# A two-layer graph network: the second layer's edge inputs laid out and loaded another way

## What is computed

```
hid = silu(edge_scalars @ fc_w1 / 8)           # edge_scalars: 100000 x 64
w   = hid @ fc_w2 / 8                          # 224 weights an edge
es, ev = h_s[src], h_v[src]                    # row src of the node table
y0, y1 = edge_attr[:, 0], edge_attr[:, 1:4]    # four factors an edge
m   = products of w, es, ev, y0 and y1         # 96 scalars, 128 vectors an edge
agg = segment_sum(m, dst)                      # over the edges of each node
```

## Time and profile before

| | us |
|---|---|
| median of 3 runs | 4200.96 |
| lowest and highest | 4200.42 and 4204.09 |
| span of the profiled execution (core 0, first to last instruction) | 4499.2 |
| PE busy in that span | 3588.3 |
| VectorE busy | 3413.8 |
| ACT busy | 3129.9 |
| POOL busy | 3025.2 |
| DMA moved, all queues | 411.01 MB |

### The profile page before, as it was taken

One profiled execution on the slowest core, in us unless ns is written; L12 is line 12 of the kernel. 1 busy time (PEld: TensorE's weight loads), 2 busy tenths in 40 slices (PEclk: granted clock), 3 DMA queues, 4 the chain that ended last, 5 costly groups with the idle time before them and its releaser, 6 DMA issues. The chain is left out here.

```text
span 4499.2 us, 96352 instructions
## 1 busy us (share of the span) xinstructions
PE 3588.3 (80%) x21340; PEld 2740.0 (61%) x21340; DVE 3413.8 (76%) x12346; ACT 3129.9 (70%) x11217; POOL 3025.2 (67%) x2469
## 2 busy tenths in 40 slices
PE   3888887887778888888778866976888888888887
PEld 3777777777777777777777766864333333333334
DVE  5777777777777777777777787875777777777775
ACT  4777777777777777777777765745666666666664
POOL 2888888888888888888888851113666666666662
PEclk7999999999999999999999998987899999999989
DMA  4443344334334334333433348962333333333333
...
DMA packets 374905, 411.01 MB, mean 91 GB/s; under 512 B 98580, under 2 KB 322580, under 8 KB 374580
## 3 DMA queue, kind: packets, MB, share of 16 engines
...
## 5 line engine op out<-in xcount | busy, mean ns | idle before, releaser
L668 POOL DMA_INDIRECT ACC<-dst_tab,idx x784 | 1308.6, 1669 | 238.9 <-issue 238.9
L733 POOL DMA_INDIRECT ACC<-hid_tab,idx x784 | 830.4, 1059 | 554.7 <-issue 352.8
L812 PE MATMUL TR<-ident,M 128*128 128x128 f32 x4704 | 675.2, 281 | 445.5 <-DVE M L1533 345.6
L657 POOL DMA_INDIRECT ACC<-src_tab,idx x784 | 790.0, 1008 | 312.7 <-issue 217.5
L812 PEld LDWEIGHTS TR<-ident,M 128*128 128x128 f32 x4704 | 525.3, 143 | 539.2 <-DVE M L1533 422.8
L1136 ACT ACTIVATE MT<-TR 128x768 f32<-128x768 f32 x784 | 600.8, 825 | 26.8 <-PE TR L812 17.8
L1125 ACT ACTIVATE ACC<-W,ACC 128x64 f32<-128x64 f32 x2352 | 571.6, 327 | 0.0
L1318 ACT ACTIVATE ACC<-TR,y 128x128 f32<-128x128 f32 (+1 forms) x1568 | 419.7, 460 | 195.5 <-remote 100.3
L861 PE MATMUL HP<-w_hv,MT 128*128 128x128 f32 x3136 | 536.5, 295 | 0.0
L836 PE MATMUL E<-w_mv,MT 128*128 128x128 f32 x3136 | 477.6, 275 | 0.0
L1009 PE MATMUL HP<-M,ohE 128*128 128x480 f32 x800 | 408.0, 636 | 43.2 <-DVE M L1856 29.9
...
## 6 DMA issues: line engine op xcount, KB each, us to landing
h_tab<-ACC SPq DMA_DIRECT2D x392, 160.0 KB
...
ACC<-src_tab,idx POOLq DMA_INDIRECT x784
ACC<-dst_tab,idx POOLq DMA_INDIRECT x784
ACC<-hid_tab,idx POOLq DMA_INDIRECT x784
...
```

Of the source, the lines that this page charges most:

```text
L657: pool.indirect_dma_start(gat0[:, v.slot8, g, :], None, src_tab.ap(), bass.IndirectOffsetOnAxis(ap=idx[:, v.sslot, c:c + 1], axis=0))\
L668: pool.indirect_dma_start(gat0[:, v.slot8, g, :], None, dst_tab.ap(), bass.IndirectOffsetOnAxis(ap=idx[:, v.sslot, c:c + 1], axis=0), comp ...
L733: pool.indirect_dma_start(gat1[:, v.slot8, g, :], None, hid_tab.ap(), bass.IndirectOffsetOnAxis(ap=idx[:, v.sslot, c:c + 1], axis=0))\
L812: ins = nc.tensor.transpose(to[:, b * G + g, :], Mt[:, g, lo:lo + w], ident[:, :])
```

## The change

Three things change in the second layer's edge loop, with their data.

- The edge scalars lie in DRAM as NS blocks of 128 rows of 512 words, one block after the other, in place of 64 long rows; e64 is loaded with an access pattern of 128 rows. Its number, size (256 KB) and order stay.
- The row numbers of all superchunks are loaded once into `dst_all` (now also `src_all`), and the factors of all superchunks once into `y_all`; SP issues both after the first layer's loop and the zero fills, before its wait for the exponentials. The loads of idx and y1 within the loop are gone, with the waits that SP had for them, and so is the tile y1.
- VectorE copies the 16 row numbers of a superchunk from `src_all` to idx (new `places1` in its stage, between products and one-hots, one superchunk ahead; the first before the loop); POOL waits for a count of these copies in place of a DMA. ACT reads its scales with `y_at`.

```
--- before.py
+++ after.py
@@ -243,12 +243,12 @@
         flag = sb("flag", [1, 1], I32)
         onec = sb("onec", [P, 1])
         dst_all = sb("dst_all", [P, NC], I32)
+        src_all = dst_all[:, :]
         dstf = sb("dstf", [P, NC])
         brk = sb("brk", [P, NC + 1])
         loc1 = sb("loc1", [P, 2, 2 * Q1])
         idx = sb("idx", [P, 2, 4 * Q], I32)
         rbf = sb("rbf", [P, 2, Q, G, P])
-        y1 = sb("y1", [P, 2, 2 * Q1 * 4])
 
         M = sb("M", [P, 2, G, MW])
         M2 = sb("M2", [P, 2, G, M0])
@@ -369,9 +369,9 @@
         LC = dict(ld=[sem(f"c_ld{u}") for u in range(4)], add=[sem(f"c_add{u}") for u in range(2)],
                   **{k: sem(f"c_{k}") for k in ("oh", "loc", "far", "oha", "one", "hx", "sc", "ev")})
 
-        LB = dict(ld=[sem(f"b_ld{u}") for u in range(2)], ix=[sem(f"b_ix{u}") for u in range(2)],
-                  ga=[sem(f"b_ga{u}") for u in range(8)], y=[sem(f"b_y{u}") for u in range(2)],
-                  **{k: sem(f"b_{k}") for k in ("fc", "hid", "w", "ws", "m", "oh", "sc", "ev", "add")})
+        s_src1, s_y1 = sem("s_src1"), sem("s_y1")
+        LB = dict(ld=[sem(f"b_ld{u}") for u in range(2)], ga=[sem(f"b_ga{u}") for u in range(8)],
+                  **{k: sem(f"b_{k}") for k in ("ix", "fc", "hid", "w", "ws", "m", "oh", "sc", "ev", "add")})
 
         def k3(t):
 
@@ -522,6 +522,8 @@
             for u in range(4):
                 sp.wait_ge(LA["st"][u], 16 * (NCH // 4))
             sp.wait_ge(s_flag, 1)
+            sp.dma_start(src_all, a["src_cols"]).then_inc(s_src1, 16)
+            sp.dma_start(y_all, a["y_cols"]).then_inc(s_y1, 16)
             general = sp.value_load(flag[0:1, 0:1], min_val=0, max_val=EP)
             with sp.If(general == 0):
                 sp.sem_inc(s_passed, 1)
@@ -584,35 +586,11 @@
                     sp.wait_ge(LB["fc"], v.quad - 1)
                 n = v.quad if not v.wide else v.data() * 2 + v.place // Q
                 n = n if v.base is None else n.with_bounds(min_val=0, max_val=NS - 1)
-                blk = a["e64T"][0:1, bass.ds(n, 1), :]
-                sp.dma_start(e64[:, v.qslot, :], bass.AP(blk.tensor, blk.offset, [[SE // 2, 2], [EP, 64], [1, SE // 2]]))\
+                sp.dma_start(e64[:, v.qslot, :], a["e64T"][bass.ds(n, 1), :, :].rearrange("n p e -> (n p) e"))\
                     .then_inc(LB["ld"][v.qslot], 16)
-
-            def places1(v, total):
-
-                if v.place or not inside(v, total):
-                    return
-                if v.sup_past(2):
-                    for i in range(Q1):
-                        u = v + (i - 2 * Q1)
-                        sp.wait_ge(LB["ga"][u.slot8], u.slot_round(16 * G, 8))
-                sp.dma_start(idx[:, v.sslot, 0:2 * Q1], a["src_cols"][:, bass.ds(v.column(0), 2 * Q1)])\
-                    .then_inc(LB["ix"][v.sslot], 16)
-
-            def factors1(v, total):
-
-                if v.place or not inside(v, total):
-                    return
-                if v.sup_past(2):
-                    sp.wait_ge(LB["ws"], v.num - Q1)
-                    sp.sem_inc(s_passed, 1)
-                sp.dma_start(y1[:, v.sslot, :], a["y_cols"][:, bass.ds(v.column(0), 2 * Q1), :].rearrange("p c k -> p (c k)"))\
-                    .then_inc(LB["y"][v.sslot], 16)
 
             def sp1(t, total):
                 scalars1(t + Q, total)
-                factors1(t + Q, total)
-                places1(t + Q1, total)
 
             def sp_1(sups, wide):
                 loop_steps(sp, Q1, sups, wide, Q1, 0, sp1)
@@ -727,7 +705,7 @@
 
                     wait(LB["m"], v.num - 3)
                 if v.place == 0:
-                    wait(LB["ix"][v.sslot], v.sup_round(16))
+                    wait(LB["ix"], v.sup + 1)
                 for g in range(G):
                     c = 2 * v.place + g
                     pool.indirect_dma_start(gat1[:, v.slot8, g, :], None, hid_tab.ap(),
@@ -1291,6 +1269,7 @@
                 if t >= 2:
                     take_n(t - 2, (3, 4))
             act.wait_ge(s_tab1d, 80)
+            act.wait_ge(s_y1, 16)
 
             def hidden(v, total):
 
@@ -1306,17 +1285,14 @@
                 if not inside(v, total):
                     return
                 act.wait_ge(LB["w"], v.num + 1)
-                if v.place == 0:
-                    act.wait_ge(LB["y"][v.sslot], v.sup_round(16))
                 if v.past(4):
                     act.wait_ge(LB["m"], v.num - 3)
                 for g in range(G):
                     wg_ = Wr[v.par][:, g, 0:224]
                     for k in range(4):
                         lo, hi = (0, 96) if k == 0 else (96, 224)
-                        c = 4 * (G * v.place + g) + k
                         ins = nc.scalar.activation(WS[v.slot][:, g, P * k:P * k + hi - lo], wg_[:, lo:hi], ACT.Copy,
-                                                   scale=y1[:, v.sslot, c:c + 1])
+                                                   scale=y_at(v, g, k))
                 ins.then_inc(LB["ws"], 1)
 
             def take_window(v, total):
@@ -1855,14 +1831,22 @@
                 TT(mid(384, (C, 3), (1, C)), fX[:, :, :, 0, :], fX[:, :, :, 1, :], ALU.subtract)
                 TT(mid(256, (C, 3), (1, C)), feat(S, (C, 3), (1, C)), wgt(64, (0, 3), (1, C)), ALU.mult).then_inc(LB["m"], 1)
 
+            def places1(v, total):
+                if v.place or not inside(v, total):
+                    return
+                nc.vector.tensor_copy(idx[:, v.sslot, :], src_all[:, columns_of(v, 0, 2 * Q1)]).then_inc(LB["ix"], 1)
+
             def stage1(t, total):
                 ch.restart()
                 products1(t, total)
+                places1(t + Q1, total)
                 one_hots1(t + 1, total)
 
             def dve_1(sups, wide):
+                places1(Step(0, None, wide, Q1), sups * Q1)
                 loop_steps(dve, Q1, sups, wide, 1, 0, stage1)
                 ch.restart()
+            dve.wait_ge(s_src1, 16)
             ch.restart()
             both(dve, dve_1)
 
@@ -1921,7 +1905,7 @@
         "dst_line": np.concatenate([dst, dst[-1:]])[None],
         "dst_rows": dst.reshape(P, NCH, G).transpose(1, 2, 0).reshape(NCH, CH),
         "src_cols": cols(src), "dst_cols": cols(dst), "y_cols": cols(y).reshape(P, NC, 4),
-        "e64T": e64.reshape(NS1, P, 2, Q, G, 64).transpose(5, 0, 2, 4, 3, 1).reshape(64, NS, SE),
+        "e64T": e64.reshape(NS1, P, 2, Q, G, 64).transpose(0, 2, 4, 5, 3, 1).reshape(NS, P, SE // 2),
         "firsts": dst.reshape(NS1, 2 * SE)[:, 0][None], "lasts": dst.reshape(NS1, 2 * SE)[:, 2 * SE - 1][None],
         "Ws_val_T": g["L0_gnn_Ws_val"].T,
         "adot_rep": np.broadcast_to(g["L0_gnn_alpha_dot"].reshape(1, S), (P, S)),
```

49 lines of the change are left out of this document (18 added, 31 removed).

## The result

The changed kernel takes 4223.62 us (median of 4 runs, 4221.39 to 4224.73) against 4202.52 (4200.42 to 4206.13) of the kernel before on the same chip: a ratio of 1.0047, 95% interval 1.0033 to 1.0061. It is slower by 21 us, where 45 us of gain were forecast, and it lies 16 us above the range.

A forecast was written before the change was run, and what follows sets the result against it. VectorE was taken to bound the second layer's edge loop, which lost 307 us against its pace in the profile. Timed sum: 4201.0 - 6 - 44 + 5 = 4156 us; range for 8 in 10: 3985 to 4208.

The forecast's parts named there:

- The bound: Second layer's edge loop: VectorE, busiest, sets the pace at 2.62 us a step, 392 x 2.62 = 1027 us.
- (1): Start of the second layer's edge loop: e64 on sixteen engines lands earlier, so VectorE starts earlier: -6 us.
- (2): Second layer's edge loop: 49 unnamed waits of VectorE go with the DMA changes; -44 us timed, bounds -5 and -165.
- Rival B: The loop's stall is the recording's alone and timed runs already go at VectorE's pace: 4200 us, chance 0.22.
- (3): 49 copies of row numbers on VectorE, one a superchunk, 0.10 us each: +5 us, bounds +2 and +25.
- (4): Row numbers and factors loaded before the loop, hidden in a DMA gap ahead of ex_tab's store: 0, without cover +6.
- (5): ACT's L1318 reads its scales in place, computing a register per instruction: cost 0, upper bound +39 us.
- (6): SP issues 98 DMAs fewer; nobody waits for SP after that except the e64 load, with a superchunk of lead.
- C: Slower: as Rival B, but VectorE sets the pace and the copy costs its upper bound, +25: 4220 us, chance 0.11.

The follow-up runs named there:

- e64: Not a run: the kernel's buffer of edge scalars, loaded by DMA in the second layer's edge loop; the change loads it as 128 rows.
- e1: The kernel before with only the new e64 layout; idx and y still come by DMA in the loop: ratio 1.0030.
- before again: The kernel before, unchanged, run and profiled a second time (also called "before, undisturbed"): ratio 0.9996, loop 1090.2 us.
- e3: The changed kernel with a second copy of the same size on VectorE, its result unused, once a superchunk: ratio 1.0057.
- e2: The changed kernel with the old load and layout of e64 put back, all the rest of the change kept: ratio 1.0049.
- e7: The kernel before with only the row numbers loaded once and copied by VectorE; y by DMA and the e64 layout as before: ratio 1.0048.
- e10: The changed kernel with the copies of the row numbers on ScalarE in place of VectorE: ratio 1.0036.
- e4: The changed kernel with SP issuing the loads of row numbers and factors behind the write of ex_tab and the wait for it: ratio 1.0050.
- e5: The changed kernel with VectorE's longest product (0.68 us) first in its step: ratio 1.0345.
- e11: e8 with VectorE's 0.68 us product ahead of the reduce and not behind it: ratio 1.0356.
- e13: The kernel before with POOL's add to agg_tab issued between the two gathers of a step, one gather later: ratio 1.0025.
- e8: e1 with an added wait: before its products VectorE also waits for the next step's gathers: ratio 1.0089.
- e9: The changed kernel with an added wait: before its products VectorE also waits for the next step's gathers: ratio 1.0083.
- e12: e1 with POOL's add to agg_tab issued between the two gathers of a step, one gather later: ratio 1.0030.
- e14 to e17: The changed kernel with POOL's add one gather later, 1.0058; then one-hots ahead of products on e12 (1.0040), on e1 (1.0033), on the kernel before (1.0022).

## Why the prediction was wrong

**The bound.** The step that failed first is the floor of the loop, which the prediction took from VectorE (392 x 2.62 = 1027 us). VectorE starts its step after 2.63 us, as read, but has 1.3 us of slack in a superchunk of 22.36; POOL has none, and its loop is the 1090 us measured. It was overlooked because the table of stretches gives POOL 871 busy us of 1334: the 0.305 us that pass ahead of each gather (239 us for 784) count as idle, although POOL can't use them. In the disturbed profile's group of these gathers "issue" stood behind 353 of the 555 us of idle time ahead of these gathers. The rule of the Trainium skill quoted above would have been a rival on the slower side, and wasn't weighed.

**(1) e64 at the loop's start.** Right: sixteen engines, 144 packets, first product 5.6 us earlier (forecast 6).

**(2) The stalls.** Wrong, and the largest term. Rival B's premise was the right one: the stalls were the recording's, all 49, and a second profile of the same kernel has none. The -44 is 0. Its upper bound of -5 excluded a loss here ("below nothing" was to be in a rival, and no rival has it), and there was one: with the faster load VectorE stands 2 us earlier against POOL, its products fall on other gathers, and e1 pays +18 us in 45 superchunks. The gather behind the add is 45 x 0.49 = 22 of them (its mean is 1.86 us, 1.37 in before again); the other gathers and POOL's shorter waits give 2 back each. That the loss comes of the load is measured (e1); that it comes by way of the phase is read from the traces, since no run set the phase back. B named the slow engines' effect on the gathers' landing and took it for a cost only; it delayed work that had slack.

**(3) Copies.** A copy took 0.36 us and not 0.10:

```profile
L1837 DVE COPY idx<-dst_all x45: 158/358/365, 3109.8 to 4117.0; 128x16 int32 x43, 128x16 int32<-128x16 int32 x2
```

It cost VectorE's step little (the next instruction starts 0.08 us behind it), and a second one cost the loop nothing (e3). The term was mis-sized without harm. What was left out is that the row numbers' part costs 12 us in the loop in e2's profile, by way of POOL's gathers again (1.040 us in the mean, 1.028 in before), and 28 in e7's, from another group of runs, 6 of them as waits of POOL; the two ratios are equal. e10 doesn't settle whether the copies' place on VectorE has a part in it; why the row numbers' part costs is open.

**(4) Loads beforehand.** Wrong: +2.6 us by ex_tab's store, not 0. The gap without transfers that was to hide them is there in before, undisturbed, too, but in that gap VectorE comes to its branch, and with the loads in flight it goes on 2.6 us later. SP itself stood 11.53 us in the first issue behind the fills. Moved behind the store, the loads cost more (e4). The bound of +6 holds.

**(5) Scales in place.** Right: ACT's 128-wide form into ACC takes 566 ns in the mean in before, undisturbed, and in after, and e7 agrees. **(6) SP.** Right that nobody waits for SP but the e64 load, but its freedom moved the two e64 loads of a superchunk by 5.5 and 9.6 us, which the sum left out.

**Rivals.** C had the sign and nearly the number (4220, measured 4223.6), with the wrong engine: a copy on VectorE didn't decide, and VectorE didn't set the pace. The chance of slower, 0.13, is C's 0.11 and 0.02 that the prediction doesn't assign; the losses that the bounds of (4) and (5) allow got no chance of their own, and for (2), where the loss came, none was allowed. That C's number is near is luck.

None of the eighteen edited or changed kernels beats the kernel before: all are at 1.0022 or more. What stays open is why VectorE and POOL settle at the phases they do. The lengths of gathers follow from the phase, but for the small phases named above; the phase, which follows from the landings and so from those lengths, came out as forecast in e5, e11 and e13 and not in e8, e9, e12 and e14 to e17.
